# Second factor of the feed-forward weights transposed by VectorE in blocks of 32, with a new order of transfers, fills, rows and factor groups in the first stage

## The chip, the cores and the metric

One core of one Trainium2 chip runs the whole program. The metric is the device time of one execution in microseconds (us), of which the runs give a median and a range. A profile of one execution gives the rows that are read below; its span is the time from the first to the last recorded instruction of that core.

## The reference, cut to what matters

X is 8 sequences of 256 tokens of 128 numbers in float32. Four blocks follow each other, each with a layer norm in front and a residual behind:

```python
x = L0_attn_a_X
x = x + attn_a(_layernorm(x), ...)   # 16 heads, differential softmax attention, causal
x = x + ffn(_layernorm(x), fc1_A, fc1_B, fc2_A, fc2_B, fc1_logits, fc2_logits)
x = x + attn_b(_layernorm(x), ...)   # linear attention
x = x + ffn(_layernorm(x), ...)      # the same weights again

def _compose_weight(logits, A, B):   # A: (32, d_in, 64), B: (32, 64, d_out)
    vals, idx = jax.lax.top_k(logits, TOP_K)
    w = jax.nn.softmax(vals / TEMPERATURE)
    return jnp.einsum('k,kir,kro->io', w, A[idx], B[idx])
```

TOP_K is 32, the number of primitives, so all are taken, and the order does not matter. The change is about the two composed weights. W1 (128x512) comes from fc1_A (32x128x64) and fc1_B (32x64x512). W2 (512x128) comes from fc2_A (32x512x64, 4.19 MB) and fc2_B (32x64x128, 1.05 MB). The sum over primitive k and rank r has 2048 terms, 16 chunks of 128, and TensorE needs k and r of A on the partitions. In memory r is the last axis of A, so A has to be transposed.

## The kernel before, in words

The first stage (project_sync, project_gpsimd, project_scalar, project_vector, project_tensor) runs over 8 sequences b. For each, VectorE normalises the rows (rows, L531), TensorE transposes them (L621), ScalarE copies the result out of PSUM (columns, L490), and TensorE projects q, k (L641) and v (L647). ScalarE casts q and k to bfloat16 (L500) and copies v (L503). VectorE forms the rest (L549) and casts it (L554, both in split), and GpSimd forms the last part (L469). The parts of one sequence go to DRAM (L423, L425) from one of three buffers (PARTS), and ScalarE may write a buffer again only when its store of three sequences before has landed (L497). The attention reads the parts back as stacks (load_stack, L267), one stack for a group of 16 maps, in four slots. GpSimd fills the stacks' rows of ones first (fill_ones, L210).

Between the projections TensorE composes the two weights. A written table, FACTORS (L295), says for each slot which factor groups are turned (ahead) and which are multiplied (behind). Slots 0 to 7 are the sequences of the first stage, and slots 8 to 13 are the first turns of the attention loop (HEAD_SLOTS is 6; function head on each engine). Group i under 4 is a quarter of the first factor: four transposes on TensorE (L354), one multiplication by the mixing weights on VectorE (L328), four products of 128x512 (L367) that accumulate in one PSUM bank. Group i from 4 to 19 is one chunk of the second factor: four transposes on TensorE (L354), scaling by the mixing weights on VectorE (L336) or ScalarE (L321), four products of 128x128 (L372). The turned chunks share the memory of a1T. VectorE copies W1 at slot 4 (L614), and ScalarE copies W2 (L898) before the attention's second pass may use that bank.

All transfers are issued by SyncE on one queue, in program order. Before the change this is: X tile 0, Wq, Wk, Wv, X tiles 1 to 3, fc1_A (L390), the logits (L392), fc1_B quarters 0 and 1 (L396), small weights, then for each sequence a wait for its parts and their store. Behind store 0 and store 1 comes an fc1_B quarter, behind store 2 fc2_B (L431), behind stores 3 and 4 an fc2_A quarter of four transfers (L404), behind stores 5 and 6 the stacks 0 and 1. Behind store 7 come fc2_A quarters 2 and 3, and then, in attend_sync, stacks 2 and 3 and the two shift rows of group 0 (L733). The attention subtracts a row maximum: units of 4 maps are scored and reduced on VectorE (L1011, L1018), after four units the maxima of a group are transposed, written by ScalarE (L890) and VectorE (L912) as shift rows, and sent into the stack by four small transfers. Only then can TensorE compute the shifted scores (L1115), in attention slot 6 (L_EXP).

## Time and profile before

| | us |
|---|---|
| median of 3 runs | 427.91 |
| lowest and highest | 423.36, 429.05 |
| the profiled execution | 427.97 |
| its span | 426.3 |
| mean granted TensorE clock over its span | 0.98 |

The profiled execution took 1.7 us more than its span, and it lies on the median. In the rows, PE is TensorE's matmuls, PEld its weight loads, DVE VectorE, ACT ScalarE, POOL GpSimd, and SPq SyncE's queue of issues. PEclk is the granted clock as a share of 2.4 GHz. The DMA share is the mean busy share of 16 engines and can be over 1, since packets overlap.

### The profile page before, as it was taken

How to read it: one execution, taken by the hardware profiler on the slowest of the kernel's cores; microseconds unless marked ns; L12 is line 12 of the kernel's file. 1: busy time of each engine (PE TensorE's matmuls, PEld its weight loads, DVE VectorE, ACT ScalarE, POOL GpSimd, SP SyncE). 2: the span in 40 equal slices, each digit the busy share in tenths (PEclk: the TensorE clock that was granted, in tenths of full speed). 3: DMA queues.
4: the chain of work that ended last, by engine and by line, in shares of the span. 5: the costliest groups of instructions: out<-in, count | busy, mean ns of one | idle time of the engine just before them, and what ended most of it. 6: DMA issues, size and time to landing. Idle time of an engine off the chain costs nothing.

```text
span 426.3 us, 10103 instructions
## 1 busy us (share of the span) xinstructions
PE 367.6 (86%) x3380; PEld 238.7 (56%) x3380; DVE 302.6 (71%) x974; ACT 241.2 (57%) x585; POOL 199.1 (47%) x319
## 2 busy tenths in 40 slices
PE   0699895397999888999899798989989989999996
PEld 0566585385555554655455555445866656664774
DVE  6586853068899789797979698785565789998110
ACT  3342341035788778787878687773755243353822
POOL 6224422002458577575858486660026667873000
PEclk9999999599899999999999999999999999999999
DMA  8879999970356425354555500000000000000011
GB/s 208 271 235 336 262 249 237 239 138 2 61 82 90 78 45 77 46 82 66 77 78 78 78 4 3 3 3 1 2 0 2 0 1 2 1 1 2 21 29 49
DMA packets 47347, 34.50 MB, mean 81 GB/s; under 512 B 20033, under 2 KB 41665, under 8 KB 47297
## 3 DMA queue, kind: packets, MB, share of 16 engines
q1 hardware_dynamic: 47296, 33.86, 37.9%
q8 instruction: 28, 0.46, 0.5%
q14 instruction: 23, 0.18, 0.2%
HBM read 25.20 MB, written 8.39 MB: 79 GB/s over the span
## 4 chain that ended last, share of the span: by engine, by line
PE 49%; DVE 17%; issue 9%; SPq 9%; ACT 6%; POOL 5%; DMA 4%; DVEq 0%; POOLq 0%; ACTq 0%
PE ps L1366 6%; PE ps L1157 5%; PE ps L1357 5%; PE ps L1081 4%; SPq L404 3%; ACT arena L823 3%; DVE arena L1499 3%; PE ps L1089 3%; DVE arena L1018 3%; DMA stacks<-arena 3%; PE ps L1076 3%; DVE arena L1512 2%; PE ps L1570 2%; PE ps L641 2%; PE ps L1233 2%
## 5 line engine op out<-in xcount | busy, mean ns | idle before, releaser
L775 POOL TENSOR_SCALAR_AFFINE_SELECT arena<-arena 128x256 f32<-128x256 f32 (+1 forms) x192 | 90.6, 486 | 93.9 <-ACT arena L823 90.1
L823 ACT ACTIVATE arena<-ps 128x512 f32<-128x512 f32 x192 | 109.3, 604 | 28.1 <-PE ps L1115 27.7
L1018 DVE TENSOR_REDUCE arena<-ps 128x4 f32<-128x1024 f32 x64 | 78.3, 1223 | 12.5 <-PE ps L1089 9.8
L1011 DVE CUSTOM_DVE_ANT_0 ps<-ps,future 128x128 f32<-128x128 f32 x256 | 66.3, 321 | 17.1 <-PE ps L1076 17.1
L1440 POOL TENSOR_TENSOR arena<-arena 128x1024 f32<-128x1024 f32 x16 | 34.2, 2136 | 38.8 <-DVE arena L1525 38.8
L1115 PE MATMUL ps<-stacks 50*128 50x256 bf16 x256 | 50.0, 275 | 0.7 <-ACT arena L823 0.7
L1081 PE MATMUL ps<-stacks 48*128 48x256 bf16 x256 | 40.5, 275 | 2.1 <-DVE arena L1018 1.7
L1157 PE MATMUL ps<-arena,values 128*17 128x256 f32 x512 | 40.5, 388 | 0.0
L469 POOL TENSOR_TENSOR qk_parts_sb<-qk_rest,qk_parts_sb 128x512 bf16<-128x512 f32 x16 | 19.1, 1211 | 40.2 <-DVE qk_parts_sb L554 40.2
L1011 DVE DVE_READ_ACCUMULATOR2_ANT arena<- 128x1 f32 x256 | 36.2, 141 | 0.1
L1570 PE MATMUL ps<-arena,upto 128*128 128x384 f32 x96 | 35.9, 486 | 0.0
L1076 PE MATMUL ps<-stacks 48*128 48x128 bf16 x256 | 25.0, 218 | 9.8 <-ACT arena L823 4.7
L1366 PEld LDWEIGHTS ps<-w,qk_parts_sb 128*128 128x128 f32 x256 | 29.4, 192 | 3.6 <-ACT qk_parts_sb L1315 2.0
L1366 PE MATMUL ps<-w,qk_parts_sb 128*128 128x128 f32 x256 | 30.2, 276 | 1.1 <-ACT qk_parts_sb L1315 1.1
L1357 PE MATMUL ps<-a1T,w 128*128 128x512 f32 x64 | 29.3, 595 | 0.9 <-issue 0.7
L1499 DVE TENSOR_TENSOR arena<-ps,arena 128x384 f32<-128x384 f32 x48 | 24.4, 547 | 6.9 <-PE ps L1570 5.8
L1315 ACT ACTIVATE qk_parts_sb<-ps 128x512 f32<-128x512 f32 x32 | 18.3, 595 | 19.5 <-PE ps L1357 19.4
L1081 PEld LDWEIGHTS ps<-stacks 48*128 48x128 bf16 x256 | 18.7, 95 | 18.7 <-DVE arena L1018 9.0
L1203 PE MATMUL ps<-ident,arena 128*128 128x128 f32 x128 | 25.6, 282 | 2.4 <-DVE arena L912 1.3
L1076 PEld LDWEIGHTS ps<-stacks 48*128 48x128 bf16 x256 | 14.8, 94 | 22.5 <-issue 15.2
L1161 PE MATMUL ps<-arena,values 128*17 128x128 f32 x512 | 26.0, 275 | 0.0
L321 ACT ACTIVATE a1T<-ps,mix_col 128x512 f32<-128x512 f32 x11 | 7.5, 687 | 32.4 <-PE ps L354 32.4
(139 smaller groups left out, 735.6 us busy)
## 6 DMA issues: line engine op xcount, KB each, us to landing
stacks<-qk_parts SPq DMA_DIRECT2D x96, 128.0 KB, 4.8
qk_parts<-qk_parts_sb SPq DMA_DIRECT2D x16, 384.0 KB, 5.2
arena<-in_L_ffn_fc_B_dram SPq DMA_DIRECT2D x4, 1024.0 KB, 7.9
arena<-in_L_ffn_fc_A_dram SPq DMA_DIRECT2D x16, 256.0 KB, 5.0
xs<-in_L_attn_a_X_dram SPq DMA_DIRECT2D x4, 256.0 KB, 4.2
qk_parts<-qk_parts_sb SPq DMA_DIRECT2D x8, 128.0 KB, 6.2
stacks<-arena SPq DMA_DIRECT2D x64, 4.0 KB
out_dram<-xs SPq DMA_DIRECT2D x4, 256.0 KB, 2.3
```

The costliest lines, as they stand in the source:

```text
L775: nc.gpsimd.affine_select(out=diag, in_=diag, compare_op=ALU.is_ge, fill=0.0, base=0, pattern=[[0, 2 if s < 2 else UMAPS], [1, P]], channe ...
L823: nc.scalar.activation(probs[:, r, s, :], ps[:, bank, :], ACT.Exp, scale=SCALE).then_inc(exp_done, 1)
L1011: last = nc.vector.tensor_tensor_reduce(out=block, in0=block, in1=future[:], scale=1.0, scalar=LOWEST, op0=ALU.add, op1=ALU.max, accum_out ...
L1018: nc.vector.tensor_reduce(out=rowmax[:, gs, 1, UMAPS * uu:UMAPS * (uu + 1)], in_=ps[:, S_BANK + 1:S_BANK + 3, :].rearrange("p b (m k) -> p ...
L1076: last = nc.tensor.matmul(bank[:, m * P:(m + 1) * P], q[:, m0 + m, 0:P], k[:, m0 + m, 0:P], start=True, stop=True)
L1081: nc.tensor.matmul(bank[:, m * SEQ:(m + 1) * SEQ], q[:, m0 + 2 * s - 2 + m, P:SEQ], k[:, m0 + 2 * s - 2 + m, :], start=(m == 0), stop=Fals ...
L1115: last = nc.tensor.matmul(bank[:, m * SEQ:(m + 1) * SEQ], k[:, m0 + 2 * s + m, 0:P], q[:, m0 + 2 * s + m, :], start=True, stop=True)
L1157: nc.tensor.matmul(ps[32 * m:32 * m + DV + 1, O_BANK + r, 0:SEQ], values[:, tile, head, :], probs[:, p, m // 2, m % 2 * SEQ:m % 2 * SEQ + ...
L1357: nc.tensor.matmul(ps[:, up_bank(S, k, c), :], w1[:, c * P:(c + 1) * P], f_xnT[:, k % 2, :], start=True, stop=True).then_inc(S["up"], 1)
L1366: last = nc.tensor.matmul(ps[:, down_bank(S, k), t * D:(t + 1) * D], hT[:, k % 2, c, t * P:(t + 1) * P], w2[:, c, :], start=(c == 0), stop ...
L1499: nc.vector.tensor_tensor(prod[:, t, EG * e:EG * e + EG, :], ps[:, 3 + (2 * EG * w + i) % 4, 0:EG * D].rearrange("p (e d) -> p e d", e=EG) ...
L1570: last = nc.tensor.matmul(bank, upto[:], rows, start=True, stop=(t == 0))
```

## The change

The second factor's chunks are no longer transposed by TensorE. fc2_A is loaded so that 32 partitions hold 8 primitives, in 16 transfers of 256 KB that each fill 32 partitions, and VectorE transposes a chunk in one instruction, as 32x32 blocks. fc2_B is loaded in the matching order, in four transfers of 32 partitions, and it carries the mixing weights now: ScalarE scales it in place, in 8 instructions, after sequence 3. The scaling by ScalarE and VectorE of the turned chunks is gone. FACTORS begins the second factor a slot earlier and has 4 head slots in place of 6.

The order of the transfers changes: the logits come before X tile 2, fc1_B is loaded whole before store 0, the fc2_A quarters come behind stores 0, 2, 3 and 4, fc2_B and the small weights behind store 1, and stacks 0 and 1 before store 5. Stacks 2 and 3 and the shift rows stay behind store 7. GpSimd fills the stacks in turns of sequences 1 to 4 in place of before sequence 0. ScalarE takes the first columns and the roots in another order, and VectorE normalises the next rows between the rests and their casts. Cut to its core:

```diff
-        FACTORS = (((0, 1), ()), ((2,), (0,)), ((3,), (1,)), ((), (2,)), ((), (3,)), ((4, 5), ()),
-                   ((6, 7, 8), (4, 5, 6)), ((9, 10, 11), (7, 8, 9)),
-                   ((12, 13), (10, 11)), ((14, 15), (12, 13)), ((16,), (14, 15)), ((17, 18), (16,)),
-                   ((19,), (17, 18)), ((), (19,)))
+        FACTORS = (((0, 1), ()), ((2,), (0,)), ((3,), (1,)), ((), (2,)), ((4, 5), (3,)), ((6, 7), (4, 5)),
+                   ((8, 9, 10), (6, 7, 8)), ((11, 12, 13), (9, 10, 11)),
+                   ((14, 15), (12, 13)), ((16, 17), (14, 15)), ((18, 19), (16, 17)), ((), (18, 19)))
...
+        def turn_factor(dve, i):
+
+            n = i - 4
+            dve.wait_ge(fc2_a_in[n // 4], 16 * P // BLK)
+            dve.wait_ge(acc_done, max(4, i - 3))
+            nc.vector.transpose(a2T[:, n % 4, :].rearrange("p (j b) -> p j b", b=BLK),
+                                a2[:, n // 2, :, BLK * (n % 2):BLK * (n % 2) + BLK]).then_inc(fT_done, 1)
+
+        def scale_second_factor(act):
+            act.wait_ge(s_mix, 9)
+            act.wait_ge(fc2_b_in, 16 * P // BLK)
+            for c in range(KR // 2):
+                nc.scalar.activation(b2[:, 2 * c:2 * c + 2, :], b2[:, 2 * c:2 * c + 2, :], ACT.Copy,
+                                     scale=mix_rows[:, c:c + 1]).then_inc(b2_scaled, 1)
...
                 if i == 4:
-                    pe.wait_ge(fc2_b_in, 16)
+                    pe.wait_ge(b2_scaled, KR // 2)
                     pe.wait_ge(w12_done, 1)
...
-                if n < len(ahead):
+                if n < len(ahead) and ahead[n] < 4:
                     factor_transposes(ahead[n])
...
-                c = slice(PRIMS // 4 * quarter, PRIMS // 4 * (quarter + 1))
-                for j in range(FCH):
-                    sp.dma_start(a2[:, j, c], fc2_A[c, j * P:(j + 1) * P].rearrange("k p r -> p k r"))\
+                for i in range(P // BLK):
+                    k = PRIMS * BLK // P * i + 2 * quarter
+                    sp.dma_start(a2[BLK * i:BLK * (i + 1), 2 * quarter:2 * quarter + 2]
+                                 .rearrange("p c j r -> p (c j) r"),
+                                 fc2_A[k:k + 2].rearrange("k (j p) r -> p (k j) r", p=BLK))\
                       .then_inc(fc2_a_in[quarter], 16)
...
+            load_rows(1)
+            for i, w in enumerate((fc1_logits, fc2_logits)):
+                sp.dma_start(logits[:, i, :], w.partition_broadcast(P)).then_inc(logits_in, 16)
+            load_rows(2)
+            load_rows(3)
+            sp.dma_start(a1, fc1_A.rearrange("k d r -> d k r")).then_inc(fc1_a_in, 16)
+            for quarter in range(4):
+                load_fc1_b(quarter)
+            store_parts(0)
+            load_fc2_a(0)
...
+            store_parts(1)
+            load_fc2_b()
...
+            store_parts(2)
+            load_fc2_a(1)
...
+            store_parts(3)
             load_fc2_a(2)
+            store_parts(4)
             load_fc2_a(3)
+            sp.wait_ge(parts_out[0], 48)
+            sp.wait_ge(stacks_filled, 4)
+            load_stack(sp, 0, 0)
+            load_stack(sp, 1, 1)
+            for b in range(5, SEQS):
+                store_parts(b)
...
-            for slot in range(4):
-                fill_ones(slot, stacks_filled)
             for b in range(SEQS):
+                if 1 <= b <= 4:
+                    fill_ones(b - 1, stacks_filled)
...
-                if b == 4:
-                    act.wait_ge(s_mix, 5)
-                scale_factors_scalar(act, b)
+                if b == 3:
+                    scale_second_factor(act)
...
             for b in range(SEQS):
-                split(b)
+                rests(b)
                 if b + 2 < SEQS:
                     rows(b + 2)
+                mids(b)
```

## Rows read from the trace of the kernel before

**Rows 1.** The page's 40 slices of the span (10.7 us each).

```profile
PE   0699895397999888999899798989989989999996
...
PEclk9999999599899999999999999999999999999999
DMA  8879999970356425354555500000000000000011
GB/s 208 271 235 336 262 249 237 239 138 2 61 82 90 78 45 77 46 82 66 77 78 78 78 4 3 3 3 1 2 0 2 0 1 2 1 1 2 21 29 49
```

**Rows 2.** Chain that ended last, 58 to 104 us: start us, us, what.

```profile
59.35 0.42 SPq L267
...
70.37 1.75 SPq L404
72.17 3.00 SPq L404
75.20 1.35 SPq L404
76.59 4.91 DMA arena<-in_L_ffn_fc_A_dram
81.55 1.11 PE ps L354 x4
```

**Rows 3.** Windows: busy us of the engines, PEclk, DMA share, GB/s.

```profile
12.00:14.00 2.00, 1.45 (x5) 1.27 (x6) 0.00 (x0) 0.84 (x4) 0.00 (x0) 1.00 0.37 91
14.00:20.00 6.00, 5.13 (x19) 3.95 (x17) 3.67 (x8) 2.43 (x8) 1.58 (x2) 1.00 1.04 361
21.50:25.50 4.00, 4.00 (x16) 2.84 (x15) 3.83 (x9) 2.16 (x5) 0.58 (x1) 1.00 0.16 40
26.00:28.00 2.00, 2.00 (x11) 1.23 (x10) 2.00 (x6) 0.00 (x0) 1.30 (x2) 1.00 1.16 348
...
71.00:81.00 10.00, 0.00 (x0) 0.00 (x0) 0.58 (x1) 0.00 (x0) 0.00 (x0) 0.58 1.14 241
76.00:84.00 8.00, 2.45 (x12) 2.45 (x13) 0.75 (x1) 0.00 (x0) 0.00 (x0) 0.50 1.23 228
86.00:92.00 6.00, 6.00 (x54) 5.26 (x53) 4.16 (x18) 1.42 (x3) 0.00 (x0) 0.98 1.05 184
94.00:99.00 5.00, 5.00 (x46) 4.26 (x45) 4.01 (x15) 1.98 (x4) 0.00 (x0) 1.00 0.01 2
```

**Rows 4.** Timeline of SyncE's issues, 41 to 101 us: start us, us.

```profile
82.33 6.29 SPq L267 DMA_DIRECT2D stacks<-qk_parts  x12
...
97.57 2.92 SPq L733 DMA_DIRECT2D stacks<-arena  x4
```

**Rows 5.** Timeline of TensorE: slot 4 begins, slot 6 begins.

```profile
95.60 0.39 PE L1076 MATMUL ps<-stacks 48*128 48x128 bf16 x4
...
101.31 0.28 PE L1115 MATMUL ps<-stacks 50*128 50x256 bf16 x1
```

**Rows 6.** Chain, 20 to 36 us: one sequence of the first stage.

```profile
27.46 0.44 PE ps L354 x4
27.89 0.22 PE ps L621 x2
28.11 1.73 PE ps L641 x8
29.84 0.86 PE ps L647 x4
30.70 3.43 PE ps L367 x8
```

**Rows 7.** Timeline of VectorE, 3 to 22 us: rows without and beside GpSimd.

```profile
8.73 0.57 DVE L538 TENSOR_SCALAR xn<-xs,moments,rstd 128x128 f32<-128x128 f32 x2
...
18.58 2.29 DVE L538 TENSOR_SCALAR xn<-xs,moments,rstd 128x128 f32<-128x128 f32 x2
```

**Rows 8.** Groups by line, 0 to 101 us: busy us, mean ns, idle before.

```profile
L321 ACT ACTIVATE a1T<-ps,mix_col 128x512 f32<-128x512 f32 x11 | 7.5, 687 | 32.4 <-PE ps L354 32.4
...
L554 DVE CAST qk_parts_sb<-qk_rest 128x512 bf16<-128x512 f32 x16 | 6.0, 419 | 0.0
...
L336 DVE TENSOR_SCALAR a1T<-ps,mix_col 128x512 f32<-128x512 f32 x5 | 3.7, 748 | 14.8 <-PE ps L354 14.8
...
L490 ACT COPY xnT<-ps 128x256 f32<-128x256 f32 x8 | 3.0, 370 | 16.4 <-PE ps L621 16.4
...
L480 ACT COPY wqk<-wqkv 128x256 f32<-128x256 f32 x2 | 1.2, 648 | 0.6 <-DMA wqkv<-in_L_attn_a_Wv_dram 0.6
```

**Rows 9.** Timeline of VectorE, 68 to 72 us: first and last step of one attention unit.

```profile
69.40 0.30 DVE L1011 CUSTOM_DVE_ANT_0 ps<-ps,future 128x128 f32<-128x128 f32 x1 [2.46 <-PE ps L1076]
...
70.36 1.22 DVE L1018 TENSOR_REDUCE arena<-ps 128x4 f32<-128x1024 f32 x1
```

**Rows 10.** The page's DMA issues: KB each, median us to landing.

```profile
stacks<-qk_parts SPq DMA_DIRECT2D x96, 128.0 KB, 4.8
...
arena<-in_L_ffn_fc_A_dram SPq DMA_DIRECT2D x16, 256.0 KB, 5.0
```

More of the change, by code:

```diff
@@ L303, in proj_bank, with scale_factors @@
             return ps[:, PROJ_BANKS[(3 * b + i) % 4], :]
-        def scaled_by_scalar(i):
-            return i >= 5 and i % 2 == 1 or i >= 14
-        def scaled_wait(eng, i):
-            if scaled_by_scalar(i):
-                eng.wait_ge(fT_done_act, sum(scaled_by_scalar(n) for n in range(i + 1)))
-            else:
-                eng.wait_ge(fT_done, sum(not scaled_by_scalar(n) for n in range(i + 1)))
-        def scale_factors_scalar(act, slot):
-            for i in FACTORS[slot][0]:
-                if scaled_by_scalar(i):
-                    act.wait_ge(fT_ps, i + 1)
-                    act.wait_ge(acc_done, max(4, i - 3))
-                    nc.scalar.activation(a2T[:, (i - 4) % 4, :], ps[:, FT_BANK + i % 2, :], ACT.Copy,
-                                         scale=mix_col[:, 1, i - 4:i - 3]).then_inc(fT_done_act, 1)
-        def scale_factors_vector(dve, slot):
+        def scale_factors(dve, slot):
             for i in FACTORS[slot][0]:
@@ L387, in project_sync, with load_rows @@
                 sp.dma_start(wqkv[:, i, :], w).then_inc(w_in, 16)
-            for i in range(1, 4):
+            def load_rows(i):
                 sp.dma_start(xs[:, 4 * i:4 * i + 4, :], x_tiles[:, 4 * i:4 * i + 4, :]).then_inc(x_in[i], 16)
-            sp.dma_start(a1, fc1_A.rearrange("k d r -> d k r")).then_inc(fc1_a_in, 16)
-            for i, w in enumerate((fc1_logits, fc2_logits)):
-                sp.dma_start(logits[:, i, :], w.partition_broadcast(P)).then_inc(logits_in, 16)
             def load_fc1_b(quarter):
@@ L475, in project_scalar, with roots @@
             load_log_exp(act)
-            for i in range(4):
-                if i == 1:
-                    act.wait_ge(w_in, 16 * 3)
-                    for side in range(2):
-                        nc.scalar.copy(wqk[:, side].rearrange("k c (d m) -> k c d m", d=DH),
-                                       wqkv[:, side].rearrange("k (c m d) -> k c d m", c=2, d=DH))\
-                            .then_inc(wqk_done, 1)
+            def roots(i):
                 c = slice(4 * i, 4 * i + 4)
@@ L490, in columns @@
                 nc.scalar.copy(xnT1[:, b % 2, :], ps[:, X_BANK, 0:SEQ]).then_inc(xnT_done, 1)
+            roots(0)
+            act.wait_ge(w_in, 16 * 3)
+            for side in range(2):
+                nc.scalar.copy(wqk[:, side].rearrange("k c (d m) -> k c d m", d=DH),
+                               wqkv[:, side].rearrange("k (c m d) -> k c d m", c=2, d=DH))\
+                    .then_inc(wqk_done, 1)
             columns(0)
+            roots(1)
             for b in range(SEQS):
@@ L576, in mixing_weights @@
                     half = slice(64 * k, 64 * k + 64)
-                    nc.vector.tensor_copy(mix_col[half], mix[half].rearrange("p i (c k) -> p i c k", k=2)[:, :, :, k])\
+                    nc.vector.tensor_copy(mix_col[half], mix[half, 0].rearrange("p (c k) -> p c k", k=2)[:, :, k])\
+                        .then_inc(s_mix, 1)
+                for i in range(P // BLK):
+                    rows = slice(BLK * i, BLK * (i + 1))
+                    nc.vector.tensor_copy(mix_rows[rows], mix[rows, 1, KR // 2 * i:KR // 2 * (i + 1)])\
                         .then_inc(s_mix, 1)
@@ L893, in head @@
             def head(slot):
-                if slot < HEAD_SLOTS:
-                    scale_factors_scalar(act, SEQS + slot)
                 if slot == HEAD_SLOTS - 1:
@@ L1046, in head @@
                 if slot < HEAD_SLOTS:
[L1047 removed]
+                    scale_factors(dve, SEQS + slot)
                 if slot == HEAD_SLOTS:
[L1049 removed]
+                    dve.wait_ge(fT_done, FGROUPS)
                     nc.vector.memset(ps[:, O_BANK:O_BANK + 2, 0:SEQ], 0.0).then_inc(cleared, 1)
```

91 lines of the change are left out of this document (38 added, 53 removed).

## The prediction

> **What bounds the kernel now.** I read the page's slices first. Up to slice 8 or 9 the DMA engines are 0.7 to 0.99 busy, and behind that they fall below 0.7. TensorE has a hole in slices 7 and 8, where its clock is low too [rows 1]. The change touches only this first quarter of the span. Next I read the chain. From 59.35 us on it runs through SyncE's issues, then through the fc2_A transfers issued from 70.37 us, and TensorE resumes at 81.55 us with the transposes of the third fc2_A quarter [rows 2]. In those 10 us TensorE does nothing, at a mean clock of 0.58, while the DMA share is 1.14 [rows 3]. So the hole is a wait for bytes, not for an engine.
>
> The windows say what the queue did. It is full until about 93.4 us and empty from 94 us. Before that it has two holes: 12 to 14 us at a share of 0.37, worth 2.0 x 0.63 = 1.3 us, and 21.5 to 25.5 us at 0.16, worth 4.0 x 0.84 = 3.4 us [rows 3]. The same windows price the kinds of transfer: fc1_B 361 GB/s, mostly parts 348, fc2_A 228, stacks 184 [rows 3]. After the queue is empty the attention still needs the shift rows, which are issued at 97.57 us [rows 4]. Slot 4 begins at 95.60 us, and the first shifted product of slot 6 at 101.31 us [rows 5], 5.7 us later. Everything behind 101.3 us is the same program before and after. So the sum is about one point, called T here: 101.3 us now, and the rest of the span, 426.3 - 101.3 = 325.0 us, stays. The profiled execution took 1.7 us more than its span (427.97 against 426.3) and lies on the median of 427.91.
>
> **The change, part by part.** *TensorE loses work.* 16 chunks of four transposes at 0.44 us [rows 6] are 7.0 us, about 3 of it in the head slots. None of it counts by itself: the hole hides it, and in the head slots VectorE's time below decides.
>
> *VectorE and ScalarE.* 11 scalings of 0.69 us leave ScalarE, and 5 of 0.75 leave VectorE [rows 8]. VectorE gets 16 block transposes of 128x512 float32, which the trace does not show. The bounds are the cast of that size in SBUF (0.42 us mean, 0.37 undisturbed) below and the TENSOR_SCALAR of that size (0.75 us) above [rows 8]. If GpSimd can hold it, the factor of the next paragraph applies in the first stage. I take 0.6 us. The Trainium skill (Vector Engine (DVE) Microarchitecture Reference, "The reshape front-end and per-opcode configuration") states one element per cycle per lane. By that it would be an estimate of 0.53 us and a start cost, which changes nothing here.
>
> ScalarE gets 8 scalings of 128x256 in SBUF. By the nearest rows (0.37 and 0.65 us [rows 8]) that is 3.0 to 5.2 us, in one piece after sequence 3, behind a wait for fc2_B. Queued behind that wait are the columns of sequence 5 and the casts of sequence 4, for which TensorE and VectorE wait. fc2_B lands at about 43 us (all of fc1_B, store 0, one fc2_A quarter, store 1 and itself come first: 27.7 us at the prices above, times the 1.08 below, from 12.8 us), so ScalarE stands until then and goes on at 46 to 48 us. Sequence 3's projection ends at 28.11 + 6.68 + 1.73 + 0.86 = 37.4 us in the trace [rows 6] and earlier after the change, so the wait is 6 us or more. Sequence 4's parts are then complete at about 53 us, and the queue comes to store 4 at about 60 us. The full queue hides it, with some 7 us to spare.
>
> *Rows before casts.* The two normalisations took 0.57 us alone and 2.29 us beside GpSimd's subtraction [rows 7]. Moved ahead of the casts they run while GpSimd is idle, which saves 1.7 us in the loop from one sequence to the next. In slots 1 to 4 TensorE is full (0.44 + 0.22 + 1.73 + 0.86 + 3.43 = 6.68 us a sequence [rows 6]), and later the queue holds. Gain: 0. The same holds for the fills and the first columns: sequence 0 gets through earlier, and its store waits behind fc1_B. What it does bring is that each store is ready before the queue comes to it, so the queue doesn't run dry.
>
> *The queue.* The bytes are the same. fc1_B quarters 2 and 3 now stand ahead of store 0 and fill the second hole, 3.4 us. The first hole follows fc1_A's transfer and may stay, so I take half of it, 0.6 us. Gain 4.0 us (bounds 3.4 and 4.7). The same prices check the model: from 26.0 us, seven stores (2.6 each), two fc1_B quarters (2.9), fc2_B (3.0), fc2_A (18.4) and four stacks (4.3) add up to 62.6 us, where the trace took 67.4, a factor of 1.08.
>
> *Narrow transfers.* fc2_A and fc2_B now go into 32 partitions at a time. The trace has no such transfer. The nearest are the stack loads, each into 16 partitions: 184 GB/s in spite of long rows. The upper bound is 228 for fc2_A and 348 for fc2_B [rows 3]. I take 206 for both, midway for fc2_A, and for fc2_B nearer to the narrow row, since it is narrow too. fc2_A: 4.19 MB / 206 = 20.4 us against 18.4 (16 transfers of 256 KB [rows 10]), fc2_B: 5.1 against 3.0. Cost 4.1 us. The ends are 0 and the 7.7 us of the first rival.
>
> *The sum.* The queue ends at 93.4 - 4.0 + 4.1 = 93.5 us. Behind it stand the shift rows. In an empty queue slot 6 began 3.7 us after the first issue at 97.57 [rows 4, 5], with 1.3 us for two issues. In a full queue SyncE issues ahead (the last stack issue ended at 88.6 us, and the queue drained at 93.4 [rows 3, 4]), so I take 1.4 us (0 to 2.4). T = 94.9 us by the queue. By the engines: stack 0 now stands ahead of three stores and three stacks (7.8 + 12.9 = 20.7 us, times 1.08 = 22.4), so it lands at 71.1 us. A unit on VectorE takes 2.2 us here (69.40 to 71.58 [rows 9]), and I take 2.5. Slots 0 to 2 take 2.5 + 2 x 0.6 = 3.7 us each and slot 3 takes 2.5. The clock adds about 1.5 us: TensorE idles before stack 0, and after the hole of before, resumed at 81.55 us, it ran at 0.50 (1.2 GHz) to 84 us at least and at 0.98 from 86 us [rows 2, 3]. Slot 4 begins at 71.4 + 11.1 + 2.5 + 1.5 = 86.5 and slot 6 at 92.2 us by the 5.7 of [rows 5]. The queue decides, by 2.7 us. T falls from 101.3 to 94.9, which is 6.4 us. Span 94.9 + 325.0 = 419.9, time 421.6 us. So of the 10.7 us hole about 4 come back as the shift rows' place in the queue.
>
> **The rivals.** *Half the ports.* A transfer into 32 partitions could go at no more than half the rate of the fastest wide one, 361 / 2 = 180 GB/s. fc2_A then takes 23.3 us (+4.9) and fc2_B 5.8 (+2.8), together 7.7. The queue ends at 97.1, T is 98.5, saving 2.8: 425.2 us. For it: the stack loads' 184. Against it: they go into 16 partitions, and fc2_A moved only 228 in wide form, near enough to such a limit to lose little. The Trainium skill (SBUF — State Buffer, "Door 1: The DMA port swizzle") states this rule against the change: 32 partitions reach 8 of 16 ports, measured there at 189 GB/s. By its rate the queue would end between this case and mine, and the trace's 184 for 16 partitions lies above the 104 that it gives for them.
>
> *Free blocks.* Narrow costs nothing and both holes go. The queue ends at 88.8, T is 90.2, the engines reach slot 6 at about 87.5, so the queue still decides. Saving 11.1: 416.9 us. For it: fc2_A is slow by its short rows, which do not change. Against it: the stacks' rate.
>
> *ScalarE's wait shows.* If fc2_B lands later or the sequences behind it go on at 6.7 us each [rows 6], the first stage ends behind stack 0. TensorE is ready at about 77 us, T = 77 + 21 = 98: 424.7 us. The 7 us to spare speak against it.
>
> *The narrow blocks multiply (slower than before).* The mechanism is one: each of the short-row transfers fills half the ports at half the rate of its wide form, 114 GB/s, and fc2_B 174. fc2_A costs 18.4 us more and fc2_B 3.0. The queue ends at 110.8, T is 112.2: 438.9 us. It becomes slower than before when both together cost over 10.5 us, which is at about 162 GB/s. Nothing in the trace goes that low: stacks with a quarter of the ports make 184.
>
> **How the numbers follow.** Forecast 421.6 us with a chance of 0.53, half the ports 0.19, free blocks 0.17, ScalarE's wait 0.06, multiplied blocks 0.05. A measurement of this kernel tells about 2% (8.6 us) from no change, so faster means below 419.3. Of the forecast's spread (417.5 to 425) about 0.17 lies below that, and with the free blocks' 0.17 that makes 0.34. Slower has the last rival, 0.05. Same has 0.61. The range goes from 415.0 (free blocks, with 0.4 us transposes and both holes) to 428.0 us (half the ports with transposes of 1.1 us, or a late ScalarE). That leaves out the last rival and the edges.
>
> **What would show each step.** Right: the DMA share near 1 from 14 us to a point at 90 to 96 us with no dip near 23 us. TensorE's wait is for a stack at 65 to 72 us, and no wait for fc2_A remains. Eight ScalarE scalings stand in one piece at 43 to 48 us behind a wait for fc2_B. Normalisations at 0.28 us each, block transposes at 0.5 to 0.75. The first L1115 product right behind the queue's end. Wrong: windows of fc2_A transfers below 190 or above 225 GB/s, the shift rows landing well before slot 6 (then the engines decide), the queue dry while SyncE waits for a sequence's parts, or stretches behind T that are not as long as before.

## The result, and the profile of the changed kernel

The changed kernel is slower by 1.15%: a median of 432.81 us of 4 runs (430.02 to 435.14) against 428.39 us of the kernel before, a ratio of 1.0115 with an interval of [1.006, 1.0171]. The forecast was 421.6 us with a range up to 428.0, so the time lies outside it, on the slow side, and it moved the other way than forecast. The profiled execution took 430.56 us and its span is 428.8 us, against 427.97 and 426.3 before. So the profile shows 2.6 of the 4.4 us between the medians. Two of the four executions took 435.1 us, at a mean granted clock of 0.939 and 0.944 where the profiled one has 0.955. No trace of such an execution was kept, and what costs them the rest isn't known.

The page's slices of the changed kernel:

```profile
PE   2899397296899989999989898989989989999996
...
PEclk9989796788799999999999999999999999999999
DMA  7999989996054544455444500000000000000011
GB/s 191 332 274 208 229 162 214 170 288 96 6 94 81 80 51 77 77 77 77 76 78 77 77 5 3 3 4 2 0 2 0 1 2 0 2 1 0 19 32 50
```

Against [rows 1], the DMA engines are now busy in all of the first nine slices and in half of the tenth, where they were done at the start of the tenth or before. At the same time they move fewer bytes a second: slices 4, 6 and 8 have 208, 162 and 170 GB/s at digits of 8 and 9. A row of 9s is not a fast queue. The first clue lies in these two lines read together.

Windows of the changed kernel (busy us and number of instructions of PE, PEld, DVE, ACT, POOL, then granted clock, DMA share, GB/s):

```profile
14.00:25.00 11.00, 8.96 (x31) 5.41 (x30) 8.44 (x22) 3.85 (x13) 5.33 (x5) 0.84 1.02 371
28.00:34.00 6.00, 6.00 (x25) 3.81 (x24) 3.17 (x7) 1.61 (x4) 3.27 (x3) 1.00 1.27 156
34.00:36.00 2.00, 2.00 (x10) 1.58 (x9) 1.23 (x2) 1.47 (x4) 0.00 (x0) 1.00 0.44 93
42.00:44.00 2.00, 2.00 (x6) 0.87 (x5) 0.00 (x0) 0.00 (x0) 0.00 (x0) 1.00 1.24 181
54.00:57.50 3.50, 3.50 (x17) 2.99 (x17) 2.16 (x5) 1.66 (x4) 1.08 (x1) 0.77 0.26 57
71.00:75.00 4.00, 4.00 (x24) 3.56 (x23) 2.89 (x6) 1.36 (x4) 1.09 (x1) 0.79 1.37 166
98.00:103.00 5.00, 3.19 (x26) 1.52 (x24) 4.85 (x21) 0.96 (x2) 0.00 (x0) 1.00 1.03 155
```

These rows answer to [rows 3]. fc1_B still goes at 371 GB/s (14 to 25 us). *Narrow* is the form of transfer that fills 32 partitions, *wide* the one that fills 128. fc2_A in its narrow form goes at 156 and 166 GB/s where it went at 228, and fc2_B at 181 GB/s (192 from 40 to 45 us). The four lambda transfers share the window of the 156. Windows that lie inside each of the four quarters have 162, 172, 170 and 165. The share of 1.27 and 1.37 says that the engines are fully loaded meanwhile. The hole at 21.5 us is gone, and a new one lies at 54 to 57.5 us (share 0.26), with a smaller one at 34 to 36 us (0.44). The queue is empty from 103.5 us, where it was from 93.4 us.

SyncE's issues in its timeline say what stands in the new hole:

```profile
46.50 4.64 SPq L389 DMA_DIRECT2D arena<-in_L_ffn_fc_A_dram  x4
51.19 4.68 SPq L431 DMA_DIRECT2D rms_col<-_L_attn_a_rms_scale_dram  x8
55.91 1.01 SPq L405 DMA_DIRECT2D qk_parts<-qk_parts_sb  x2
...
71.32 8.18 SPq L269 DMA_DIRECT2D stacks<-qk_parts  x12
...
91.81 6.12 SPq L269 DMA_DIRECT2D stacks<-qk_parts  x12
100.26 2.89 SPq L741 DMA_DIRECT2D stacks<-arena  x4
```

Eight transfers of one small column take 4.68 us to issue. The fc2_A bytes issued before them run out in this time, and nothing else stands in the queue. The last line is [rows 4]'s shift rows: issued at 100.26 us, 2.69 us later than before, behind stacks 2 and 3.

The chain that ended last, 75 to 106 us:

```profile
75.97 8.04 DMA stacks<-qk_parts
84.05 0.60 PE ps L1082 x4
...
100.26 0.82 SPq L741
101.14 3.62 DMA stacks<-arena
```

TensorE's timeline at the points of [rows 5], the first attention unit and the first shifted product:

```profile
84.05 0.60 PE L1082 MATMUL ps<-stacks 48*128 48x128 bf16 x4 [7.61 <-DMA stacks<-qk_parts]
...
104.89 0.26 PE L1082 MATMUL ps<-stacks 48*128 48x128 bf16 x1 [2.42 <-DMA stacks<-arena]
104.90 0.39 PE L1121 MATMUL ps<-stacks 50*128 50x256 bf16 x1
```

The wait for fc2_A in [rows 2] is gone. TensorE waits 7.61 us for stack 0 instead, and 2.42 us for the shift rows. T, the first shifted product, is at 104.9 us, where it was at 101.3. Behind it stand 428.8 - 104.9 = 323.9 us, before 325.0. So the 2.5 us of the span are 3.6 us lost ahead of T and 1.1 us won behind it, and everything that follows is about the first 105 us of the profiled executions.

The small steps, in the timelines of ScalarE, TensorE and VectorE:

```profile
46.42 3.30 ACT L330 ACTIVATE arena<-arena,mix_rows 128x256 f32<-128x256 f32 x8 [10.07 <-DMA arena<-in_L_ffn_fc_B_dram]
```

```profile
52.43 0.66 PE L629 MATMUL ps<-ident,xn 128*128 128x128 f32 x2 [7.08 <-DVE xn L539]
```

```profile
14.00 0.59 DVE L539 TENSOR_SCALAR xn<-xs,moments,rstd 128x128 f32<-128x128 f32 x2
...
52.87 1.30 DVE L323 STREAM_TRANSPOSE a1T<-arena 128x512 f32<-128x512 f32 x2
```

ScalarE stands 10.07 us for fc2_B and TensorE 7.08 us behind it, as forecast. A normalisation takes 0.30 us and a block transpose 0.65 us.

### The profile page after: what moved, and what is told of

Its sections match the earlier page's. It is cut to its first block, busy times and chain, and to the rows that moved or that the text cites. A ratio compares the mean times of both kernels' runs of the same rounds, so it can differ in the third digit from the quotient of the medians.

```text
span 428.8 us, 9985 instructions
## 1 busy us (share of the span) xinstructions
PE 369.7 (86%) x3316; PEld 236.9 (55%) x3316; DVE 301.0 (70%) x989; ACT 236.4 (55%) x582; POOL 198.7 (46%) x319
## 4 chain that ended last, share of the span: by engine, by line
PE 47%; DVE 15%; SPq 10%; issue 9%; ACT 7%; POOL 6%; DMA 4%; DVEq 0%; POOLq 0%; ACTq 0%
PE ps L1372 6%; PE ps L1163 6%; PE ps L1363 5%; PE ps L1087 5%; ACT arena L831 3%; SPq L389 3%; DVE arena L1024 3%; DVE arena L1505 3%; PE ps L1095 3%; PE ps L1082 2%; DVE arena L1518 2%; PE ps L1167 2%; PE ps L1576 2%; PE ps L1209 2%; PE ps L1239 2%
## 5 line engine op out<-in xcount | busy, mean ns | idle before, releaser
L1087 PE MATMUL ps<-stacks 48*128 48x256 bf16 x256 | 41.6, 280 | 2.9 <-DVE arena L1024 1.9
L468 POOL TENSOR_TENSOR qk_parts_sb<-qk_rest,qk_parts_sb 128x512 bf16<-128x512 f32 x16 | 19.1, 1210 | 49.7 <-DVE qk_parts_sb L557 49.7
L1095 PE MATMUL ps<-future_bf,ident_bf 128*128 128x256 bf16 x128 | 25.8, 284 | 0.0
```

What stands on the lines that cost most here:

```text
L1087: nc.tensor.matmul(bank[:, m * SEQ:(m + 1) * SEQ], q[:, m0 + 2 * s - 2 + m, P:SEQ], k[:, m0 + 2 * s - 2 + m, :], start=(m == 0), stop=Fals ...
L1095: nc.tensor.matmul(bank.rearrange("p (m k) -> p m k", m=2)[:, :, P:SEQ], ident_bf[:], future_bf[:], start=False, stop=True, skip_group_che ...
```

## The experiments

Two theories stood at first. *Narrow cost*: the transfers into 32 partitions cost far more than 4.1 us. *Dry queue*: the moved small transfers open as much as the new order closes. Two more came from the trace: ScalarE's 10 us stall (*stall*), and stack 0's late landing (*stack*). In the table "end" is where the windows show the queue empty, to about half a microsecond, "slot 0" is the first attention unit on TensorE, and T is as above. The experiments were run in three sets, each beside the kernel before: its median was 428.02 us in the set of e1 to e4, 427.44 in that of e5 to e8, 428.21 in that of e9 to e11. The ratio compares executions that ran side by side, so it isn't exactly the quotient of these medians, and between sets it is the ratios that compare. The last three columns come from one profiled execution each.

| kernel | median us | ratio to before, interval | end | slot 0 | T |
|---|---|---|---|---|---|
| changed | 432.81 | 1.0115 [1.006, 1.0171] | 103.5 | 84.1 | 104.9 |
| e1_wide | 424.76 | 0.9937 [0.9889, 0.9985] | 94.0 | 75.5 | 95.6 |
| e2_rms | 426.32 | 0.9954 [0.9914, 0.9994] | 97.0 | 78.9 | 98.3 |
| e3_both | 419.26 | 0.9781 [0.9695, 0.9866] | 90.0 | 73.3 | 91.7 |
| e4_before_narrow | 431.92 | 1.0085 [1.0044, 1.0126] | 93.5 | | 103.9 |
| e5_late | 432.11 | 1.0087 [1.0038, 1.0136] | 104.2 | 84.3 | 106.4 |
| e6_stack0 | 435.69 | 1.0138 [1.0066, 1.0209] | 106.2 | 77.4 | 107.8 |
| e7_contig | 414.52 | 0.9617 [0.9536, 0.9697] | 84.5 | 71.2 | 88.0 |
| e8_contig_late | 414.06 | 0.9622 [0.953, 0.9713] | 85.0 | 67.1 | 86.6 |
| e9_shift_first | 431.11 | 1.0101 [1.0038, 1.0163] | | 75.8 | 100.8 |
| e10_before_rms | 428.72 | 1.0019 [0.9991, 1.0047] | 90.0 | | 100.7 |
| e11_best | 411.91 | 0.9624 [0.9571, 0.9677] | | 65.7 | 82.5 |

### e1_wide: the same bytes at the same places in the queue, into 128 partitions

```diff
-                for i in range(P // BLK):
-                    k = PRIMS * BLK // P * i + 2 * quarter
-                    sp.dma_start(a2[BLK * i:BLK * (i + 1), 2 * quarter:2 * quarter + 2]
-                                 .rearrange("p c j r -> p (c j) r"),
-                                 fc2_A[k:k + 2].rearrange("k (j p) r -> p (k j) r", p=BLK))\
+                c = slice(PRIMS // 4 * quarter, PRIMS // 4 * (quarter + 1))
+                for j in range(FCH):
+                    sp.dma_start(a2[:, 2 * quarter + j // 2, 8 * (j % 2):8 * (j % 2) + 8],
+                                 fc2_A[c, j * P:(j + 1) * P].rearrange("k p r -> p k r"))\
...
-                for i in range(P // BLK):
-                    k = PRIMS * BLK // P
-                    sp.dma_start(b2[BLK * i:BLK * (i + 1)],
-                                 fc2_B[k * i:k * (i + 1)].rearrange("k (e p) f -> p (k e) f", p=BLK))\
+                for i in range(4):
+                    sp.dma_start(b2[:, 4 * i:4 * i + 4],
+                                 fc2_B[8 * i:8 * i + 8].rearrange("k r f -> (k r) f").rearrange("(c p) f -> p c f", p=P))\
```

> The changed kernel, but fc2_A and fc2_B come in transfers of 128 partitions again (same bytes, same number of transfers, same rows of 256 and 512 bytes). The numbers of the second factor then lie at other places than the transposes take them for, so W2 is not the reference's. Theory queue: in the changed kernel's trace fc2_A moves at about 162 GB/s against 228 before and fc2_B at 192 against 348, which is 7.5 + 2.5 = 10 us of a full queue. They go: the queue ends at about 93.5 us in place of 103.5, the first shifted product comes at about 96 in place of 105 us, and the time is about 9 us below the changed kernel's 432.8, so 423 to 425 us. Rival ScalarE: the 10 us in which ScalarE stands for fc2_B, TensorE idles and its clock falls are what costs; fc2_B still comes behind the same transfers, so the time falls by 3 us at most.

Measured: 424.76 us, 8.1 below the changed kernel. Its windows:

```profile
28.00:32.00 4.00, 4.00 (x18) 2.63 (x17) 1.17 (x3) 0.51 (x2) 3.27 (x3) 1.00 1.21 237
49.00:51.00 2.00, 1.17 (x4) 1.10 (x5) 2.00 (x7) 0.38 (x2) 0.90 (x1) 0.50 1.27 222
51.50:54.00 2.50, 2.50 (x10) 2.03 (x9) 1.34 (x3) 1.11 (x2) 0.98 (x1) 0.73 0.13 29
```

fc2_A is back at 237 and 222 GB/s, with the same number of transfers, the same 256 KB in each and the same rows of 256 bytes. The order in which a transfer reads DRAM changed with its form. The queue ends 9.5 us earlier, but not all of that is the narrow form. Added up from the start (mean GB/s of the window times its length), 17.5 MB, which is about the end of fc2_A, have moved at 76.7 us in the changed kernel and at 70.4 here: 6.3 us. By 23.0 MB it is 9.2 us (101.8 against 92.6). In between lie stores and the stack loads, which the edit doesn't touch. The loads of stacks 2 and 3, in the changed kernel, here, and in e3_both (below):

```profile
95.00:103.00 8.00, 6.19 (x52) 4.03 (x50) 7.85 (x32) 0.96 (x2) 0.00 (x0) 1.00 1.03 153
86.50:93.50 7.00, 5.08 (x42) 3.35 (x40) 6.85 (x31) 0.96 (x2) 0.00 (x0) 1.00 1.02 177
84.00:89.50 5.50, 4.21 (x35) 2.58 (x33) 5.35 (x25) 0.96 (x2) 0.00 (x0) 1.00 1.03 229
```

The same transfers go at 153, 177 and 229 GB/s. So the narrow form costs some 6 us up to the end of fc2_A, 1.5 times the 4.1 of the prediction, and whether the slower stack loads behind it are its doing isn't shown. The third row of the windows above shows the new hole (share 0.13), which is still there.

### e2_rms: the eight transfers of the column made into one

```diff
-            for i in range(P // DV):
-                sp.dma_start(rms_col[DV * i:DV * (i + 1), :],
-                             rms_scale.rearrange("(p a) -> p a", a=1)).then_inc(rms_in, 16)
+            sp.dma_start(rms_col[:], bass.AP(rms_scale.tensor, rms_scale.offset, [[0, P // DV], [1, DV], [1, 1]]))\
+              .then_inc(rms_in, 16 * P // DV)
```

> The changed kernel with rms_scale loaded by one transfer in place of eight of 64 bytes each. Theory queue: the eight issues take 4.7 us of SyncE in which almost no byte is queued, and the queue runs dry from 54.2 to 57.5 us (2.6 us lost). The hole goes and everything behind it comes 2 to 3 us earlier: queue end about 101 us, time about 430 us. Rival: the hole is a wait for a sequence's parts or for the engines, and the time stays at 432.8 within 1 us.

Measured: 426.32 us, 6.5 below the changed kernel, and a queue that ends 6.5 us earlier. The direction is as the dry queue says, the size is more than twice the expected. The issue (SyncE's timeline), and the windows:

```profile
51.72 0.77 SPq L430 DMA_DIRECT2D rms_col<-_L_attn_a_rms_scale_dram  x1
```

```profile
54.00:57.50 3.50, 3.50 (x13) 2.88 (x12) 2.07 (x5) 1.21 (x3) 1.62 (x2) 0.67 1.20 286
28.00:34.00 6.00, 6.00 (x26) 4.18 (x25) 2.57 (x6) 2.00 (x5) 3.27 (x3) 1.00 1.28 170
69.00:73.00 4.00, 4.00 (x24) 3.61 (x23) 2.11 (x5) 1.82 (x4) 0.32 (x1) 0.88 1.32 187
```

The issue takes 0.77 us in place of 4.68, and the hole moves 286 GB/s. The hole accounts for 2.6 us (3.5 us at a lack of 0.74). At 17.5 MB this kernel is 3.6 us ahead of the changed one, at 23.0 MB 6.3 us, so most of the remainder arises behind fc2_A, where the stack loads go at 172 GB/s (89.5 to 96.5 us) against 153. The narrow transfers themselves are much the same: windows inside the quarters have 165, 166, 181 and 173 GB/s, against 162, 172, 170 and 165, and the 170 and 187 above hold other bytes too. What sets the speed of the stack loads from one execution to the next isn't known.

### e3_both: e1 and e2 together

> Both edits: transfers of 128 partitions for fc2_A and fc2_B (W2 is not the reference's) and one transfer for rms_scale. Theory queue: the gains add up, 12 to 13 us of queue, first shifted product at 92 to 94 us, time 420 to 421 us, unless the engines decide before that: from stack 0's landing to slot 6 they need some 21 us. Rival ScalarE: at most 3 to 4 us below 432.8.

Measured: 419.26 us, ratio 0.9781 [0.9695, 0.9866], T at 91.7 us, queue end 90.0. With it the four kernels make a square, in us at 17.5 MB (about the end of fc2_A) and of the queue's end:

| | eight rms transfers | one |
|---|---|---|
| narrow | 76.7, 103.5 | 73.1, 97.0 |
| wide | 70.4, 94.0 | 67.4, 90.0 |

At 17.5 MB wide saves 6.3 or 5.7, one rms transfer 3.6 or 3.0, both 9.3. At the queue's end wide saves 9.5 or 7.0, one rms transfer 6.5 or 4.0, both 13.5. The surplus of 3 to 4 us lies in the stack loads and stores behind fc2_A. With both flaws away the changed kernel takes 2.2% less than the kernel before, though in this form its W2 is a wrong one, so this is a time and not yet a kernel. TensorE's work, ScalarE's stall and the order of the transfers are unchanged in it.

### e4_before_narrow: the kernel before, with fc2_A in the narrow form alone

```diff
-                c = slice(PRIMS // 4 * quarter, PRIMS // 4 * (quarter + 1))
-                for j in range(FCH):
-                    sp.dma_start(a2[:, j, c], fc2_A[c, j * P:(j + 1) * P].rearrange("k p r -> p k r"))\
+                for i in range(4):
+                    k = 8 * i + 2 * quarter
+                    sp.dma_start(arena[32 * i:32 * i + 32, A2_AT + 2048 * quarter:A2_AT + 2048 * (quarter + 1)]
+                                 .rearrange("p (c r) -> p c r", r=R),
+                                 fc2_A[k:k + 2].rearrange("k (j p) r -> p (k j) r", p=32))\
```

> The kernel before, where only the fc2_A transfers are narrow: 32 partitions each, 16 transfers of 256 KB as in the changed kernel; TensorE still transposes and takes the chunks from the places that a quarter fills, so W2 is not the reference's. Theory queue: each quarter takes about 6.4 us in place of 4.6, so the third quarter, on which TensorE resumes at 81.55 us, lands 5 to 6 us later, at about 87 us, and the time rises from 428.4 to about 434 us. Rival (a narrow transfer is hidden, or its low rate in the changed kernel comes from what it stands beside): within 2 us of the kernel before.

TensorE's transposes take the chunks from the new places (not shown).

Measured: 431.92 us, 3.9 slower than before, with nothing else of the change in it. Its window over the stretch for which [rows 3] has 228 GB/s, and TensorE's resumption, at 81.55 us in [rows 2]:

```profile
76.00:84.00 8.00, 1.91 (x9) 1.91 (x10) 0.75 (x1) 0.00 (x0) 0.00 (x0) 0.50 1.36 165
```

```profile
82.09 1.11 PE L356 MATMUL ps<-ident,arena 128*128 128x128 f32 x4 [9.83 <-DMA arena<-in_L_ffn_fc_A_dram]
```

The rate of 165 GB/s is confirmed in the other kernel. But the third quarter lands only 0.5 us later, not the 5 to 6 expected, and the queue ends at 93.5 us as before: what the narrow quarters lost, the transfers between and behind them won back. T is 2.6 us later, and TensorE's clock explains the other 2.0. The granted clock was 0.50 until 86.3 us in the kernel before and until 91.1 us here. From the resumption to the third attention unit TensorE takes 9.88 us here (to 91.97) against 7.88 (to 89.43), and from there to T 11.89 against 11.88.

### e5_late: ScalarE's scalings after sequence 4

```diff
-                if b == 3:
+                if b == 4:
                     scale_second_factor(act)
...
-                if b == 3:
+                if b == 4:
```

The second edit moves VectorE's small weights, which wait in the same place.

> The changed kernel, but ScalarE's eight scalings of fc2_B and VectorE's lambdas come one sequence later, after sequence 4, so that neither engine stands about 10 us for transfers (ScalarE for fc2_B to 46.4 us, VectorE for Wo to 47.4 us) while sequence 4 is behind it. Theory queue: the stall was hidden by the full queue; stack 0 and the queue's end stay within 1.5 us of 84 and 103.5 us, and the time stays within 2 us of the changed kernel's. Rival ScalarE and clock: TensorE doesn't idle from 45 to 52 us, its clock doesn't fall there, and the time falls by 4 us or more.

Measured: 432.11 us against 432.81, ratios 1.0087 and 1.0115, no difference that the runs can tell. TensorE's 7 us wait at 45 us is gone from this kernel's timeline (5.20 us for L330's result at 47 us stand in its place), and slot 0 stays at 84.3 us. The stall was hidden, as the prediction had it.

### e6_stack0 and e9_shift_first: stack 0 earlier, then the shift rows earlier too

e6_stack0 loads stack 0 ahead of the fourth fc2_A quarter. e9_shift_first is e6_stack0 with group 0's shift rows issued ahead of stack 3.

```diff
-            load_fc2_a(3)
...
             load_stack(sp, 0, 0)
+            load_fc2_a(3)
...
-            load_stack(sp, 3, 3)
             store_shift(0, 0)
+            load_stack(sp, 3, 3)
```

> The changed kernel with stack 0 issued before the last fc2_A quarter in place of behind it. The attention then begins some 6 us earlier (at about 77 to 78 us in place of 84). Theory place in the queue: the shift rows are still behind the last stack, whose place does not change, so the first shifted product stays at 103 to 105 us and the time within 2 us of the changed kernel's. Rival engines: slot 6 comes some 21 us after stack 0 whatever the queue holds, so T falls to about 99 us and the time by 5 to 6 us.

> The run with stack 0 ahead of the last fc2_A quarter, and now the shift rows of group 0 are issued before stack 3 in place of behind it. There the shift rows were computed at 94.4 us, were issued at 99.98 and landed behind the queue's end at 106.2 us, with the first shifted product at 107.8. Theory place in the queue: they are issued at about 97 us and land some 5 us earlier, first shifted product at 102 to 103 us, and the time falls by 4 to 5 us from 435.7 to about 431 us. Rival (what comes first is given back, since stack 3 is late for slot 12): the time stays within 2 us of 435.7.

Measured: e6_stack0 435.69 us, e9_shift_first 431.11. SyncE's timeline and TensorE's first shifted product of e6_stack0:

```profile
93.05 6.88 SPq L269 DMA_DIRECT2D stacks<-qk_parts  x12
99.98 2.87 SPq L741 DMA_DIRECT2D stacks<-arena  x4
```

```profile
107.80 0.26 PE L1082 MATMUL ps<-stacks 48*128 48x128 bf16 x1 [11.28 <-DMA stacks<-arena]
```

and of e9_shift_first:

```profile
92.00 3.26 SPq L269 DMA_DIRECT2D stacks<-qk_parts  x6
95.30 2.88 SPq L741 DMA_DIRECT2D stacks<-arena  x4
98.22 2.80 SPq L269 DMA_DIRECT2D stacks<-qk_parts  x6
```

```profile
100.76 0.26 PE L1082 MATMUL ps<-stacks 48*128 48x128 bf16 x1 [6.65 <-DMA stacks<-arena]
```

In e6_stack0 slot 0 begins 6.6 us earlier than in the changed kernel, and it buys nothing. T is 2.9 us later, outside the 103 to 105 us expected, with the queue's end 2.7 us later. TensorE's wait moves to the shift rows and is 11.28 us long. The rows were computed at 94.4 us, but SyncE came to them at 99.98, behind two stacks. Issued ahead of stack 3 they let T come 7.0 us earlier, while the span of the profiled execution falls by 3.6 us (431.7 to 428.1), so a part is given back behind T, where stack 3 lands later. The medians fall by 4.6 us but come from two sets, and the ratios, 1.0138 and 1.0101, have intervals that overlap: T is shown to come earlier, the gain in time isn't shown clear of noise. The wait for stack 0, the largest in the changed kernel's chain, was not what set the end.

### e7_contig and e8_contig_late: whole rows, one transfer a quarter

fc2_A is taken in the order of its memory: of each block of 4 primitives, partition q gets the q-th run of 1024 elements, 4 KB. The transposes read every second element of a row, the mixing weights are laid out to match, and the columns of W1 are permuted in its copy.

```diff
-                for i in range(P // BLK):
...
+                sp.dma_start(a2[:, 2 * quarter:2 * quarter + 2].rearrange("p c j r -> p c (j r)"),
+                             fc2_A.rearrange("k f r -> (k f r)").rearrange("(g q x) -> q g x", q=P, x=1024)
+                             [:, 2 * quarter:2 * quarter + 2]).then_inc(fc2_a_in[quarter], 16)
...
-                                a2[:, n // 2, :, BLK * (n % 2):BLK * (n % 2) + BLK]).then_inc(fT_done, 1)
+                                a2[:, n // 2].rearrange("p j (b e) -> p e j b", e=2)[:, n % 2]).then_inc(fT_done, 1)
...
+                    nc.vector.tensor_copy(w1[:].rearrange("k (j p) -> k j p", p=BLK),
+                                          ps[:, ACC_BANK, :].rearrange("k (p j) -> k j p", p=BLK))\
```

e7_contig also has fc2_B as one transfer and the one rms transfer of e2_rms, and e8_contig_late adds the edit of e5_late.

> The changed kernel with another order of the second factor's rows: partition 32i+p holds primitive 4g+i and the 16 columns 16p to 16p+15, which lie one behind the other in memory, so that a quarter of fc2_A is one transfer of 128 partitions with rows of 4 KB, and fc2_B is one transfer with rows of 1 KB. W1's columns are copied in the matching order, the block transposes take every second element, and rms_scale is one transfer. Theory queue: fc2_A moves at 350 GB/s or more, 12 us in place of 25.9, and the queue ends at 84 to 87 us; the first stage's engines decide then, since in the run with both edits TensorE was already ready no earlier than stack 0 (73.3 us). First shifted product at 85 to 89 us, time 413 to 417 us. Rival (strided reads make the transposes slow): transposes of 1.2 us or more, time above 419 us.

> The same with the scalings and the lambdas one sequence later. With the queue no longer the bound, the stall of ScalarE and VectorE for fc2_B and the small weights should show: 2 to 4 us faster than without the move, 411 to 414 us. If the first stage is still held by the queue, the same time within 1.5 us.

Measured: 414.52 and 414.06 us. A window of e7_contig:

```profile
26.00:30.00 4.00, 4.00 (x12) 2.05 (x12) 2.33 (x6) 1.23 (x3) 1.75 (x2) 1.00 1.10 375
```

The group of its block transposes, 0 to 105 us:

```profile
L323 DVE STREAM_TRANSPOSE a1T<-arena 128x512 f32<-128x512 f32 x16 | 10.2, 682 | 0.0
```

fc2_A goes at 375 GB/s with rows of 4 KB. The transposes read every second element now and take the same mean, 682 ns. In the changed kernel that group has 682 as well. The queue ends 5.5 us earlier than in e3_both, the median falls by 4.7 us, and the ratio from 0.9781 to 0.9617. In e7_contig T is 3.5 us behind the queue's end, so the engines decide, and there e8_contig_late's earlier slot 0 could count. T falls by 1.4 us, but the medians differ by less than their spread: the 2 to 4 us expected of it didn't show.

### e10_before_rms: the kernel before with one rms transfer

> The kernel before with rms_scale loaded by one transfer in place of eight. Theory queue: the hole at 21.2 to 25.8 us (3.6 us lost) stands behind these eight issues, but the store behind it waits for sequence 0's parts at 21.96 us, so only a part goes: the queue ends 1 to 3 us earlier and the time is 426 to 428 us. Rival (the hole was the missing fc1_B transfers alone): no change within 1 us.

Measured: 428.72 us, ratio 1.0019 [0.9991, 1.0047]. Its window over the hole of [rows 3]:

```profile
21.50:25.50 4.00, 4.00 (x16) 2.79 (x15) 3.86 (x8) 1.90 (x5) 0.84 (x1) 1.00 0.71 175
```

The share rises from 0.16 to 0.71 and the queue ends at 90.0 us, 3.4 earlier. So most of the hole of before was the same eight issues. And the time stays, as the rival had it, though for another reason. TensorE gets the third fc2_A quarter at 79.05 us, 2.5 us earlier than before, and has the turned chunks left to do behind it, so T is 10.7 us behind the queue's end. Of the 2.5 us it gives back 1.8 to its clock, which was 0.50 until 87.7 us here: from the resumption to the third attention unit it takes 9.72 us (to 88.77) against 7.88, and from there to T 11.89 us as before. T is 0.65 us earlier.

### e11_best: e8_contig_late with the shift rows ahead of stack 3

> The contiguous layout with the later scalings and lambdas, and the shift rows of group 0 issued before stack 3. Theory: the shift rows were computed at 81.0 us there and their product came at 86.6, 1.6 us behind the queue's end. Issued into a queue without stack 3 they land about 3.5 us after they are computed: first shifted product at 84.5 to 85 us, time 412 us, 1.5 to 2 us below 414.1. Rival: the engines decide already and the time stays at 414.

Measured: 411.91 us, ratio 0.9624 [0.9571, 0.9677], 20.9 us below the changed kernel, T 4.1 us earlier than in e8_contig_late. SyncE's timeline, with the shift rows at 79.67 us where the changed kernel has 100.26, and TensorE's first shifted product:

```profile
79.67 2.73 SPq L737 DMA_DIRECT2D stacks<-arena  x4
82.84 2.70 SPq L269 DMA_DIRECT2D stacks<-qk_parts  x6
```

```profile
82.50 0.39 PE L1117 MATMUL ps<-stacks 50*128 50x256 bf16 x1
```

It has the lowest median of all versions. Its ratio is that of e8_contig_late (0.9622) and of e7_contig (0.9617), so the runs don't tell the three apart.

## Why the prediction was wrong

The model was T = end of the queue + 1.4, with the rest unchanged. **That frame held**, in the profiled executions. T is 104.9 - 103.5 = 1.4 us behind the queue's end, and in e1, e2, e3, e5, e6 and e8 1.3 to 2.2. The rest behind T is 323.4 to 327.3 us in all kernels, 325.0 before (the largest in e8, e9 and e11, where T is early or the shift rows pass a stack). Before, T stood 101.3 - 93.4 = 7.9 us behind the queue's end, since TensorE had chunks to turn after the last bytes. So the change wins 6.5 us there, as forecast. The queue's end was forecast at 93.5 us and is 103.5. That is the miss as far as the trace shows it: T 3.6 us later in place of 6.4 earlier.

Two terms of that sum failed, and a third stood in no term.

**Narrow transfers, 4.1 us forecast, 5.7 to 6.3 measured at the end of fc2_A, 7.0 to 9.5 at the queue's end** (the square of e3_both). The mechanism was right and the size off. By the windows it looks like more: fc2_A at 162 GB/s takes 25.9 us, 7.5 more than the 18.4 of before, and fc2_B at 192 takes 5.5, 2.5 more, 10.0 together. e4_before_narrow shows why such a sum isn't the cost: at 165 GB/s for fc2_A its queue ended as before. I took 206 GB/s for the pair, between the stacks' 184 and fc2_A's wide 228, and called the worst case unlikely because "nothing in the trace goes that low". That reading was wrong. The trace of before goes lower in a full queue, while stack 0 lands:

```profile
62.00:66.00 4.00, 4.00 (x32) 3.82 (x32) 2.05 (x4) 2.38 (x5) 1.61 (x2) 1.00 1.03 150
```

The stack loads made 150 to 184 GB/s there, so the 184 was the upper end of the nearest row. fc2_A also has short rows, and narrow and short together went at 156 to 172: below the 220 to 238 of short rows in wide form (e1_wide). I had this case as a rival, with a turning point at about 162 GB/s, and gave it 0.05. Its price of 114 GB/s was too low, its turning point was where the kernel landed. Rows that each have one of two handicaps don't bound a transfer that has both. The forecast had fc2_B landing at about 43 us, from 27.7 us of transfers. Its own prices give 27.0 with narrow rates, and the landing came at 46.4.

The Trainium skill (SBUF — State Buffer, "Door 1: The DMA port swizzle") gives 189 GB/s for 32 partitions at 1 MiB. Here, in transfers of 256 KB, fc2_B, with rows of 512 bytes, went at 181 to 192, in agreement, and fc2_A, with rows of 256, at 156 to 172, below it. The Trainium skill (DMA: Bandwidth & Descriptors, "Specifications") asks for at least 512 bytes for the full rate. The trend from fc2_A to fc2_B, and from 228 GB/s to 375 in e7_contig, agrees with that, though the transfers of e7_contig are also four times as large.

**Holes filled, -4.0 us forecast, +0.6 measured** (e1_wide ends at 94.0 us, before at 93.4). The step said that fc1_B ahead of store 0 fills the second hole and that the queue doesn't run dry. The old hole was filled, and it opened again 30 us later. For the most part it had never been store 0's: [rows 3] shows the share of 0.16 at 21.5 us, and SyncE's timeline of before has eight rms issues directly ahead of it:

```profile
18.25 3.67 SPq L416 DMA_DIRECT2D rms_col<-_L_attn_a_rms_scale_dram  x8
21.96 1.01 SPq L423 DMA_DIRECT2D qk_parts<-qk_parts_sb  x2
```

I priced small transfers by bytes, which gives nothing, and not by issues, 0.42 us each. e10_before_rms shows the link from one side, e2_rms from the other. The order of the transfers as such brought no visible gain in the queue's end: e3_both and e10_before_rms, with the new order and the old, both end at 90.0 us, to within what the stack loads vary.

**Stack loads, no term forecast, up to 3 us.** The forecast left them as they were, at 184 GB/s, and they went at 153 in the changed kernel. Between 17.5 and 23.0 MB it takes 2.9 us more than e1_wide and 2.7 more than e2_rms, for the same transfers. 93.4 + 0.6 + 9.5 = 103.5 us adds up by its making, since the 9.5 holds whatever e1_wide and the changed kernel differ in, the stack loads too.

**What came as forecast.** The wait for fc2_A is gone. ScalarE's stall was forecast to end at 46 to 48 us and its eight scalings end at 49.7. It stays hidden (e5_late), store 4 going out at 62.4 us where the queue came to it. *ScalarE's wait shows* is refuted. A block transpose takes 0.65 us in a pair and 0.68 in the mean, forecast 0.6. The normalisations take 0.30 us. From slot 0 to T the forecast had 92.2 - 71.4 = 20.8 us by the engines, and it is 104.9 - 84.05 = 20.9. But slot 0 was forecast at 71.4 us and came at 84.1, by the same terms. That the 1.4 us behind the queue's end came out to the tenth is partly luck, since the other kernels have 1.3 to 2.2. *Free blocks* is refuted by the windows. *Half the ports*, at 7.7 us, lies between the two measures of the narrow cost and has the holes wrong like the forecast.

**Open.** Why a narrow transfer with 256-byte rows goes at 156 to 172 GB/s. e1_wide changes the number of partitions and the order of the reads in DRAM together, and no run has narrow transfers with long rows, so neither the ports nor the short rows are shown as the cause by themselves. fc2_A and fc2_B were not made wide one at a time. Why the same stack loads go at 150 to 229 GB/s isn't known. The lambdas' four transfers at 34 us weren't merged.

## What to carry to other kernels

Price each transfer by its form: partitions, row length, and number of issues. A small transfer costs SyncE the same 0.42 us as a large one that finds room in the queue, and eight in a row can drain the queue.

Take the lowest rate of the nearest row in a full queue as well as a typical one, before a rival is called unlikely by it.

When VectorE is to transpose in blocks of 32, choose the order of the summed index so that one transfer fills 128 partitions with long rows. With the one rms transfer this turned a kernel 1.15% slower than before into one 3.8% faster (e7_contig).

The longest wait in the chain isn't always the one that decides. Starting the attention 6.6 us earlier gained nothing while four small transfers stood behind two stacks, and moving those four ahead of one stack brought T 7.0 us earlier.

An earlier landing can be given back to the clock. In e10_before_rms TensorE resumed 2.5 us earlier at the half clock and reached T 0.65 us earlier.

## What the runs showed of the hardware that was not expected

Transfers of 256 KB into 32 partitions with 256-byte rows went at 156 to 172 GB/s in the changed kernel and at 165 to 181 in e2_rms, at a DMA share of 1.27 to 1.37. The same bytes into 128 partitions went at 220 to 238 in e1_wide, and with 4 KB rows at 375.

Loads of 128 KB into 16 partitions each went at 150 to 229 GB/s in a full queue, in kernels that issue the same ones: 150 and 184 before, 153 in the changed kernel, 177, 172 and 229 in e1_wide, e2_rms and e3_both.

A block transpose of 128x512 float32 has the same mean with contiguous and with stride-2 input, 682 ns.

Tiny VectorE instructions can be long while GpSimd is busy, in VectorE's timeline of the changed kernel:

```profile
15.97 2.36 DVE L575 TENSOR_SCALAR mix<-lg_exp,lg_inv 128x32 f32<-128x32 f32 x2
...
63.63 1.12 DVE L600 SCALAR_TENSOR_TENSOR lam<-lam_exp 128x16 f32<-128x16 f32 x1
```

They write 16 and 32 elements a partition and take 1.1 and 1.2 us, as long as a whole reduction of [rows 9]. In the kernel before, with GpSimd idle, the pair of the first line takes 0.39 us (20.98 us) and the other 0.16 (40.67). The profile's chain runs through the first pair, but whether it costs anything there wasn't tested.

TensorE's granted clock fell to 0.50 (1.2 GHz) at 79.5 us, in the 7.61 us in which TensorE waited for stack 0, and stayed there for 10.2 us. It fell again at 103.4 us, in the wait for the shift rows, for as long, and it had been at 0.50 from 48.8 to 55.6 and from 65.8 to 72.7 us too. The rest behind T was not longer for it (323.9 us against 325.0).
